# Both layer norms' roots in one GpSimd pair of operations, normalised rows from one ScalarE activation, expert weights on VectorE

## The reference

```python
# x, ctx: (64, 64, 256); 16 heads of 16; only the image branch has keys, since 64 <= 257
def layernorm(x): return (x - mean(x)) / sqrt(var(x) + 1e-5)
def rms_norm(x, w): return x * rsqrt(mean(x * x) + 1e-6) * w

h = layernorm(x)
q = rms_norm(h @ q_w.T + q_b, norm_q_w)
k = rms_norm(ctx @ k_img_w.T + k_img_b, norm_k_img_w)
v = ctx @ v_img_w.T + v_img_b
x = x + (softmax(q k^T / 4) v) @ o_w.T + o_b            # per head

h = layernorm(x)
logits = h @ gate_w.T                                   # 8 experts
topw, sel = top_k(softmax(logits), 2); topw /= topw.sum()
gate, up = split(h @ w1[e].T)                           # 2 * 176 columns, e in sel
x = x + sum over the two e of topw[e] * ((silu(gate) * up) @ w2[e].T)
```

## Time and profile before

| | before |
|---|---|
| median of three runs | 485.4 us (483.75 to 485.8) |
| the profiled execution: its time, its span | 485.2 us, 483.5 us |
| PE / PEld busy | 438.5 (91%) / 383.3 (79%) |
| DVE / ACT / POOL busy | 388.1 (80%) / 276.5 (57%) / 308.7 (64%) |
| mean granted TensorE clock | 0.984 |
| chain that ended last | PE 48%, POOL 24%, issue 13%, DVE 12% |

### The profile page before, as it was taken

How to read it: one execution, slowest core, us unless ns; L and a number is a source line. 1 busy time by engine, 2 the same in 40 slices (tenths; PEclk the granted TensorE clock), 3 DMA queues, 4 the chain that set the end, 5 groups by cost and what they waited for, 6 DMA issues and landing times.

```text
span 483.5 us, 15249 instructions
## 1 busy us (share of the span) xinstructions
PE 438.5 (91%) x4428; PEld 383.3 (79%) x4428; DVE 388.1 (80%) x1336; ACT 276.5 (57%) x802; POOL 308.7 (64%) x529
## 2 busy tenths in 40 slices
PE   7898999999999999889999998889999999998980
PEld 3567888878887887778888886679999999898870
DVE  7544888888888898898998978778876767899893
ACT  5353667666665666656666653365566656655650
POOL 6842547887888878777788786576444444444451
PEclk9997999999999999999999999999999999999996
DMA  7253443233232332423333322545444445789964
GB/s 206 82 142 82 140 141 111 87 108 95 81 114 85 104 94 86 118 75 94 104 93 92 105 86 75 148 162 166 133 132 123 127 128 153 240 254 316 309 201 157
DMA packets 55514, 64.62 MB, mean 134 GB/s; under 512 B 9599, under 2 KB 49034, under 8 KB 55434
## 3 DMA queue, kind: packets, MB, share of 16 engines
q1 hardware_dynamic: 44602, 42.59, 31.9%
q0 software_dynamic: 6480, 16.85, 9.8%
q10 hardware_dynamic: 4352, 4.20, 2.5%
HBM read 32.73 MB, written 23.14 MB: 116 GB/s over the span
## 4 chain that ended last, share of the span: by engine, by line
PE 48%; POOL 24%; issue 13%; DVE 12%; ACT 1%; DMA 1%; POOLq 1%; DVEq 0%; ACTq 0%; SPq 0%
PE bank L1351 9%; PE bank L1352 8%; PE bank L1353 8%; POOL sorted_rows L542 7%; PE bank L1592 4%; POOL r_qk L498 3%; POOL we_l L490 3%; POOL ct_l L484 2%; POOL rstd L498 2%; PE bank L1412 2%; PE bank L1625 2%; PE bank L1624 2%; PE bank L1614 2%; PE bank L1613 2%; POOL row L527 1%
## 5 line engine op out<-in xcount | busy, mean ns | idle before, releaser
L614 POOL DMA_INDIRECT expert_out<-probs,late x71 | 72.7, 1024 | 75.1 <-ACT probs L800 70.3
L542 POOL DMA_INDIRECT sorted_rows<-row,place_i x64 | 69.0, 1079 | 33.4 <-POOL row L534 14.8
L1351 PE MATMUL bank<-we_h,xt_h 128*128 x142 | 51.7, 364 | 0.8 <-DVE xt_l L1265 0.8
L705 ACT ACTIVATE probs<-bank 128x1024 f32<-128x1024 f32 x32 | 32.8, 1026 | 23.4 <-PE bank L1465 21.5
L1352 PE MATMUL bank<-we_l,xt_h 128*128 x142 | 45.8, 323 | 0.0
L1353 PE MATMUL bank<-we_h,xt_l 128*128 x142 | 45.7, 322 | 0.0
L788 ACT ACTIVATE xn<-bank 128x176 f32<-128x176 f32 x71 | 22.6, 318 | 37.4 <-PE bank L1353 37.3
L1275 DVE SCALAR_TENSOR_TENSOR probs<-xn,late,bank 128x128 f32<-128x128 f32 x71 | 24.5, 345 | 20.9 <-ACT xn L788 20.2
L932 DVE TENSOR_REDUCE bank<-bank 128x16 f32<-128x1024 f32 x32 | 39.1, 1223 | 2.0 <-PE bank L1400 2.0
L498 POOL TENSOR_TENSOR rstd<-veps,half_neg 128x1 f32<-128x1 f32 x64 | 36.6, 572 | 5.3
L800 ACT COPY probs<-bank 128x256 f32<-128x256 f32 x71 | 26.4, 372 | 18.7 <-PE bank L1625 17.2
(11 more groups left out here) (234 smaller groups left out, 1597.0 us busy)
## 6 DMA issues: line engine op xcount, KB each, us to landing
late<-sorted_rows SPq DMA_DIRECT2D x71, 129.0 KB, 2.4
we_f<-w_exp SPq DMA_DIRECT2D x32, 152.0 KB
v_bd<-v_sb SPq DMA_DIRECT2D x128, 34.0 KB
ctx_in<-ctx_t SPq DMA_DIRECT2D x32, 128.0 KB, 2.4
qp<-q_hl SPq DMA_DIRECT2D x128, 32.0 KB
x<-x SPq DMA_DIRECT2D x3, 1024.0 KB, 5.7
row<-expert_out SPq DMA_DIRECT2D x6, 512.0 KB, 5.1
qp<-expert_out SPq DMA_DIRECT2D x6, 512.0 KB, 4.4
```

The costliest lines, as they stand in the source:

```text
L542: pool.indirect_dma_start(sorted_rows, bass.IndirectOffsetOnAxis(ap=place_i[:, t.slot // 2, k, t.par:t.par + 1], axis=0), row[:, k, t.slot ...
L614: pool.indirect_dma_start(expert_out, bass.IndirectOffsetOnAxis(ap=hs(r)[:, D:D + 1].bitcast(U32), axis=0), y_sb[:, r % YRING, :], None, b ...
L1351: pe.matmul(dst, a_h, b_h, start=start, stop=False)
```

## The change

- GpSimd: `ln1` and `ln2` go. `ln_roots` in their place runs once a turn, as the turn's first work, over two columns: tile i+2's first norm and tile i-4's second norm. It is four operations: variance plus epsilon, minus the mean, the power, and their product (the shift). `weights` leaves GpSimd.
- VectorE: `ln2_norm` goes. `ln1_stats` and `ln1_mean` run three tiles ahead instead of two. `choose`, `route` and the three operations of `weights` (with a reciprocal in place of the power) now stand before `att_lo`, and `k_scale` before `gate_of_x`.
- ScalarE: `row_copy` goes. `rows_norm` reads x1 and writes both copies of the row, 128x2x256, with scale and bias read from a column.
- Rings of eight (`RSTDS`) hold the roots and shifts.

```diff
--- before.py
+++ after.py
...
-        def ln1(t):
-            need_alone(pool, pool_passed, S["xn_ready"], t.n - 1)
-            inv_sqrt(t, rstd[:, t.slot, :], veps[:, t.slot, :], mean_var[:, t.par, 1:2], 1.0, 1e-5,
-                     S["ln1_mean"], S["ln1_veps"], S["ln1_rstd"])
-            need_alone(pool, pool_passed, S["ln1_rstd"], t.n + 1)
-            pool.tensor_scalar(shift[:, t.par, :], mean_var[:, t.par, 0:1], rstd[:, t.slot, :], -1.0, ALU.mult, ALU.mult
-                               ).then_inc(S["ln1_shift"], 1)
+        def ln_roots(one, two):
+
+            cols = slice(0 if one.live else 1, 2 if two.live else 1)
+            par, ring, done_ = one.par, one.ln1, one.n + 1
+            if one.live:
+                pool.wait_ge(S["ln1_mean"], one.n + 1)
+            if two.live:
+                pool.wait_ge(S["ln2_mean"], two.n + 1)
+            pool.tensor_scalar(veps[:, ring, cols], mean_var[:, par, cols, 1], 1.0, 1e-5, ALU.mult, ALU.add
+                               ).then_inc(S["ln_veps"], 1)
+            need(pool, S["xn_ready"], min(one.n - 1, NT))
+            need(pool, S["row2_ready"], one.n - 7)
+            pool.tensor_scalar(mean_neg[:, ring, cols], mean_var[:, par, cols, 0], -1.0, None, ALU.mult
+                               ).then_inc(S["ln_mean_neg"], 1)
+            pool.wait_ge(S["ln_veps"], done_)
+            pool.tensor_tensor(rstd[:, ring, cols], veps[:, ring, cols], half_neg[:, cols], ALU.pow
+                               ).then_inc(S["ln_rstd"], 1)
+            pool.wait_ge(S["ln_rstd"], done_)
+            pool.wait_ge(S["ln_mean_neg"], done_)
+            pool.tensor_tensor(shift[:, ring, cols], mean_neg[:, ring, cols], rstd[:, ring, cols], ALU.mult
+                               ).then_inc(S["ln_shift"], 1)
...
-        def ln2(t):
-            need_alone(pool, pool_passed, S["row_ready"], t.n - 1)
-            inv_sqrt(t, rstd2[:, t.slot, :], veps2[:, t.par, :], mean_var2[:, t.par, 1:2], 1.0, 1e-5,
-                     S["ln2_mean"], S["ln2_veps"], S["ln2_rstd"])
-
-        def weights(a, b, pp):
-
-            need_alone(pool, pool_passed, R["e_gap_ready"], (a.pair + 1) * 2)
-            need_alone(pool, pool_passed, S["row2_ready"], b.n + 1)
-            w = row[:, :, a.slot:a.slot + 2, D + 1:D + 2].rearrange("p k m d -> p k (m d)")
-            pool.tensor_scalar(one_e[:, :], e_gap[:, pp, :], 1.0, 1.0, ALU.mult, ALU.add).then_inc(R["weight_set1"], 1)
-            need_alone(pool, pool_passed, R["weight_set1"], a.pair + 1)
-            pool.tensor_tensor(w[:, 0, :], one_e[:, :], one_neg[:, :], ALU.pow).then_inc(R["weight_set2"], 1)
-            need_alone(pool, pool_passed, R["weight_set2"], a.pair + 1)
-            pool.tensor_tensor(w[:, 1, :], e_gap[:, pp, :], w[:, 0, :], ALU.mult).then_inc(R["weight_set3"], 1)
...
         def turn(j, s):
+            if Tile(j, s + 2).live or Tile(j, s - 4).live:
+                ln_roots(Tile(j, s + 2), Tile(j, s - 4))
             if Tile(j, s + 1).live:
                 ctx_lo(Tile(j, s + 1))
             if Tile(j, s - 7).live:
                 send(Tile(j, s - 7), 1)
             if Tile(j, s).live:
                 qk_rms(Tile(j, s))
-            if Tile(j, s + 2).live:
-                ln1(Tile(j, s + 2))
-            if s % 2 == 0 and Tile(j, s - 6).live:
-                weights(Tile(j, s - 6), Tile(j, s - 5), (s - 6) // 2 % 2)
             if Tile(j, s - 6).live:
                 set_ids(Tile(j, s - 6))
                 send(Tile(j, s - 6), 0)
-            if Tile(j, s - 3).live:
-                ln2(Tile(j, s - 3))
...
-        ln1(Tile(0, 0))
-        ln1(Tile(0, 1))
+        ln_roots(Tile(0, 0), Tile(0, -6))
+        ln_roots(Tile(0, 1), Tile(0, -5))
...
-        def row_copy(t):
-
-            act.wait_ge(S["row_ready"], t.n + 1)
+        def rows_norm(t):
+
+            act.wait_ge(S["ln_shift"], t.n + 7)
             if t.quads_ok:
-                act.wait_ge(row_sent[1][t.slot], t.quad * 16)
-            act.copy(row[:, 1, t.slot, 0:D], row[:, 0, t.slot, 0:D]).then_inc(S["row2_ready"], 1)
+                for sent in row_sent:
+                    act.wait_ge(sent[t.slot], t.quad * 16)
+            act.activation(row[:, :, t.slot, 0:D], x1[:, t.n:t.n + 1, :].to_broadcast([P, 2, D]), ACT.Identity,
+                           bias=shift[:, t.ln2, 1:2], scale=rstd[:, t.ln2, 1:2]).then_inc(S["row2_ready"], 1)
...
-                row_copy(tile(4))
+                rows_norm(tile(4))
...
-            need(dve, S["row_ready"], t.n - 1)
+            if t.n >= 2:
+                dve.wait_ge(S["ln_shift"], t.n + 5)
             need_alone(dve, dve_passed, S["ln2_stats"], t.n + 1)
-            dve.bn_aggr(mean_var2[:, t.par, :], stats2[:, t.par, :]).then_inc(S["ln2_mean"], 1)
-
-        def ln2_norm(t):
-            dve.wait_ge(S["ln2_rstd"], t.n + 1)
-            if t.quads_ok:
-                dve.wait_ge(row_sent[0][t.slot], t.quad * 16)
-            dve.tensor_scalar(row[:, 0, t.slot, 0:D], x1[:, t.at, :], mean_var2[:, t.par, 0:1], rstd2[:, t.slot, :],
-                              ALU.subtract, ALU.mult).then_inc(S["row_ready"], 1)
...
+        def weights(a, b, pp):
+
+            dve.wait_ge(R["e_gap_ready"], (a.pair + 1) * 2)
+            w = row[:, :, a.slot:a.slot + 2, D + 1:D + 2].rearrange("p k m d -> p k (m d)")
+            dve.tensor_scalar(one_e[:, :], e_gap[:, pp, :], 1.0, None, ALU.add).then_inc(R["weight_set1"], 1)
+            dve.wait_ge(R["weight_set1"], a.pair + 1)
+            dve.reciprocal(w[:, 0, :], one_e[:, :]).then_inc(R["weight_set2"], 1)
+            dve.wait_ge(R["weight_set2"], a.pair + 1)
+            dve.tensor_tensor(w[:, 1, :], e_gap[:, pp, :], w[:, 0, :], ALU.mult).then_inc(R["weight_set3"], 1)
...
-            ahead = tile(-2) if tile(-2).live else None
+            ahead = tile(-3) if tile(-3).live else None
...
+            if isinstance(j, int) and j == s == 0:
+                ln1_stats(tile(-2), x_second)
+                ln1_mean(tile(-2))
             if ahead:
-                n = j * SKEW + s + 2 if isinstance(j, int) else None
-                ln1_stats(ahead, {2: x_second, 8: x_third, 9: x_rest}.get(n))
+                ln1_stats(ahead, {8: x_third, 9: x_rest}.get(ahead.n))
                 ln1_mean(ahead)
-            if tile(4).live:
-                ln2_norm(tile(4))
-            if tile(3).live:
-                att_lo(tile(3))
             if s % 2 == 1 and tile(5).live:
                 a = tile(5)
                 a.first = isinstance(j, int) and a.n == 0
                 choose(a, tile(4), (s - 5) // 2 % 2)
             if s % 2 == 0 and tile(6).live:
                 route(tile(6), tile(5), (s - 6) // 2 % 2)
+                weights(tile(6), tile(5), (s - 6) // 2 % 2)
+            if tile(3).live:
+                att_lo(tile(3))
             if isinstance(j, int) and j == s == 0:
                 fold_gate()
             if tile(0).live:
+                k_scale(tile(0))
                 gate_of_x(tile(0))
-                k_scale(tile(0))
                 q_scale(tile(0))
...
             route(a, b, a.pair % 2)
+            weights(a, b, a.pair % 2)
...```

The table of waits for x keeps its two numbers, 8 and 9, while the turn in which they are met is one earlier. Each of the following pieces is the order of instructions on one engine, with the semaphores that an instruction waits for. VectorE, turn 6, from the statistics that run ahead to the key's scale: before,

```order
L907 BN_STATS stats<-x 128x6 [waits x_third]
L912 BN_AGGR mean_var<-stats 128x2 [waits ln1_stats,xn_ready]
L1000 TENSOR_SCALAR row<-x,mean_var,rstd 128x256 [waits ln2_rstd]
L963 TENSOR_TENSOR at_l<-bank,at_h 128x256 [waits o_projected,at_h_ready]
L1029 TENSOR_TENSOR place<-bank,filled 128x16 [waits routed]
```

More of the change, by code:

```diff
@@ L54 @@
 SKEW = 4
+RSTDS = 8
 LAST = NT + 7
@@ L68, in __init__ @@
         self.live = not isinstance(j, int) or 0 <= self.n < NT
+        self.ln1 = (self.n - 2) % RSTDS
+        self.ln2 = (self.n + 4) % RSTDS
         self.twins = j * 2 + s // 2
@@ L114, in build_in @@
     half_neg = sb("half_neg", [P, 2], F32)
-    one_neg = sb("one_neg", [P, 2], F32)
     zero_one = sb("zero_one", [2, 2], F32)
@@ L134, in build_in @@
     stats = sb("stats", [P, 2, 6], F32)
[L135 to L138, removed]
+    mean_var = sb("mean_var", [P, 2, 2, 2], F32)
+    veps = sb("veps", [P, RSTDS, 2], F32)
+    rstd = sb("rstd", [P, RSTDS, 2], F32)
+    shift = sb("shift", [P, RSTDS, 2], F32)
+    mean_neg = sb("mean_neg", [P, RSTDS, 2], F32)
     xn = sb("xn", [P, 2, D], F32)
@@ L287, in build_in @@
     fold_ready, gate_done = sem("fold_ready"), sem("gate_done")
-    names = """ln1_stats ln1_mean ln1_veps ln1_rstd ln1_shift xn_ready x_transposed xt_h_ready xt_l_ready
+    names = """ln1_stats ln1_mean ln_veps ln_rstd ln_mean_neg ln_shift xn_ready x_transposed xt_h_ready xt_l_ready
         ct_h_ready ct_ready k_projected projected v_ready q_squared k_squared qk_veps qk_rstd qn_ready kn_ready
```

(32 more changed lines are left out.)

3 lines of the change are left out of this document (removed).

## The result

The changed kernel takes 487.44 us (median of 7 runs, 485.74 to 489.88) against 484.1 (7 runs, 483.55 to 485.8) for the kernel before on the same chip: ratio 1.007, interval 1.0039 to 1.01. It is 0.7% slower. The profiled execution took 487.44 us, its span 485.7 us, 2.2 more than the span before.

What follows compares the result with a forecast made beforehand. GpSimd was taken to bound the first part from turn 7, PE the second; -6.9 + 0.2 + 1.35 + 3.8 + 3.0 + 1.0 + 0.85 = +3.3 on 485.2 gave 488.5 us, range 482.5 to 492.5.

Steps and rivals of the forecast that it cites:

- GpSimd falls below the tensor engine: GpSimd's work from turn 7: 17.43 to 15.1 us a pair, 7.5 a turn, under the tensor engine's 7.99.
- Pairs of 16.84: Turns from 7 on: odd 8.14 and even 8.70 us, as `rows_norm` and `gap_exp` delay `k_hi`.
- Rival 1: ScalarE's delay in the turns is hidden, only `gap_exp` is left: pair 16.3, 482.1 us; chance 0.15.
- rival 3: No gain in the pairs, late `att_lo` or GpSimd behind VectorE: pair near 17.4, 495.4 us; chance 0.17.
- The wait for x, +3.8: Turn 6: VectorE waits for both loads on `x_rest`, so `project_out` comes 3.8 us late (3.2 to 4.3).
- the clock, +3.0: After turn 6's idle stretch the tensor engine's clock falls to 0.50, costing 3.0 us (0 to 3.4).
- Rival 2: x loads early enough or clock stays: 484.5 to 485.6 without the fall, 481.7 also without the wait; chance 0.13.
- 25 turns, -6.9: Turns 7 to 32: 13 odd and 12 even turns plus planning steps take 211.8 us against 218.7.
- planning steps: VectorE's planning work behind turns 21 to 24, until now mostly hidden by GpSimd, costs 1.6 us in all.
- Start, +1.35: `ln_roots` of tile 2 stands before the first `r_qk`: 1.15 us, plus 0.2 for two set-up operations.
- The rule against the change: Row's normalisation: a Trainium skill puts multiplying and adding on VectorE; followed, `k_hi` would not be late, giving Rival 1's time.
- End of the first part, +0.85: Turn 32: late `k_hi` on VectorE's chain, 0.3 us, and `weights` behind `route_last`, 0.55.

Runs made afterwards that it cites:

- e5_pool_extra: e1_split plus one idle power over two columns on GpSimd in every turn: 483.78 us, ratio 0.9997 to the kernel before.
- e7_weights_only: The kernel before with only the three operations of `weights` moved from GpSimd to VectorE: 482.64 us, ratio 0.9974.
- e9_weights_order: e7_weights_only plus VectorE's new order (choosing, routing, weights before `att_lo`; key's scale before the gate's): 475.7 us, ratio 0.9819 to the kernel before.
- e10_order_only: The kernel before with VectorE's new order alone, `weights` left on GpSimd: 482.82 us, ratio 0.9969.
- e4_act_order: e1_split with `rows_norm` and `gap_exp` issued on ScalarE after the next turn's `k_hi` and `xt_hi`: 475.07 us, ratio 0.9828 to the kernel before.
- e1_split: The changed kernel with a semaphore for each of the last two loads of x, waited for at tiles 16 and 24: 481.57 us, ratio 0.9947.
- e6_best: e4_act_order with `ln_roots` of turn 0 issued after `qk_rms`: 472.82 us, ratio 0.9782 to the kernel before.
- e2_before_wait: The kernel before with one wait added, VectorE waiting for both loads on `x_rest` in turn 6: 490.49 us, ratio 1.0128.
- e3_rows_dve: e1_split with the row's normalisation back on VectorE, ahead of `choose` and `route`, and its copy on ScalarE: 476.86 us, ratio 0.9856 to the kernel before.

## Why the prediction was right, and which steps were not

The forecast was 488.5 and slower by 0.6%; measured are 487.44 and 0.7%. Step by step:

- **GpSimd falls below the tensor engine**: right. `ln_roots` takes 1.42 for the 1.4 forecast, and with 0.69 more a turn the pairs don't move (`e5_pool_extra`). That VectorE's order was the second condition was in the forecast for the odd turn only ("`choose` made that `tr_k` 0.5 late"); `e7_weights_only`, `e9_weights_order` and `e10_order_only` show it for both turns.
- **Pairs of 16.84**: 16.90 measured, odd 8.18 for 8.14, even 8.72 for 8.70. Its cause, ScalarE's `rows_norm` (0.81) and `gap_exp` ahead of `k_hi`, is shown by `e4_act_order`: without them there 7.97 and 8.15. `tr_q` stood for `k_lo` 17 times, 0.44 in even turns, and not in nearly all turns. Rival 1, that this delay is hidden, falls, and so does rival 3, pairs near 17.4.
- **The wait for x, +3.8, and the clock, +3.0**: right in kind and place. Against `e1_split` turn 6 is 3.39 longer, turn 7 2.42 and turn 8 0.1: 5.9 for 6.8. PE stood 3.19 us, and the low clock covers 75.2 to 82.0 us, for the forecast's 74 to 81. The forecast took 64.75 for the start of turn 6 where the trace has 64.90, which makes its own term 3.7. Rival 2 gave 481.7 for a kernel without the wait; `e1_split` measured 481.57.
- **25 turns, -6.9**: mis-sized. With the clock's part of turn 7 (2.4 to 2.8) taken off they give -3.6 to -4.0. Pairs account for 0.8 of the missing 3; 1.7 is the term "1.6 for all" of the **planning steps**: turns 22 to 25 are 2.7 above two pairs and turn 29 is 0.6 above its like, 3.3 in all. The forecast let part of them fall on time that `k_hi` costs already. But turns 22 to 25 take the same 36.54 us in the changed kernel and in `e4_act_order`, where `k_hi` is on time: VectorE sets them.
- **Start, +1.35**: 1.54, and `e6_best` gives back 1.3 of it. **Start clock, +1.0**: absent in this execution (turn 1 took 7.18). It is real but irregular: `e1_split` and `e5_pool_extra` take 8.24 and 8.26 there, 1.1 more.
- **Turn 3, no term**: the forecast kept the low clock of turn 3, 2.9 us. PE's timeline of the changed kernel has 1.68 us of idle time there instead of 2.32, the clock stayed at 1.00, and 3.4 us came back:

```profile
39.15 0.64 PE L1400 MATMUL bank<-late,qp 128*64 128x128 f16 x16 [1.68 <-issue]
```

  The other kernels fall into the same two groups: before, `e2_before_wait`, `e7_weights_only` and `e10_order_only` stand 1.99 to 2.32 us there, work on at 0.50, and turn 3 takes 11.6 to 13.2; the eight others stand 0.58 to 1.82, stay at 1.00, and take 8.7 to 10.0. The seven with `ln_roots` are all among these eight, but so is `e9_weights_order`, which has none of it. With one traced execution of each kernel it is not shown which part of the change spares the stall, or how.
- **The rule against the change** (the row on VectorE would give rival 1's time, 6.4 less): by `e3_rows_dve` against `e1_split` it gives 4.7 less, but `e4_act_order`, with the row on ScalarE in another place, gives 6.5 less.
- **End of the first part, +0.85**: 1.65. The transposes of the first expert slot start 0.85 late, as forecast, its first expert matmul 1.2, and a short stretch at 0.50 (321 to 324.5 us) adds the rest.

So the total was closer than its terms: planning steps (+1.7), pairs (+0.8) and the end (+0.8) were under-estimated, and turn 3 (-3.4) and the start clock (-1.0), which have nothing to do with them, made up for it. That the total came out within 1.1 us is luck; the pairs, the wait for x and the start are not.

## What to carry to other kernels

When work moves one stage earlier, look at every semaphore that counts for several transfers: the 5.9 us here hung on a count of 32 at a tile that needs neither of the two loads counted. When two engines are nearly as late as each other, relieving one alone, or reordering the other alone, measures as next to nothing (0.3% each, 1.8% together), so try them as a pair before dropping either. An operation that another engine awaits should be issued ahead of one that nobody awaits, which was worth 6.5 us on ScalarE at unchanged durations.
